# Features and keys by column, both ends reordered, and 64 spare transposes in the first tile, in a two-layer graph attention kernel

## The reference, cut to what matters

```python
def layer0(input, W, a, adj):
    h = input @ W
    e = leaky_relu((h @ a_src)[:, None] + (h @ a_dst)[None, :], 0.2)
    valid = (adj > 0) & (h.sum(axis=1) != 0)[None, :]
    att = softmax(where(valid, e, NEG), axis=1)
    L = valid.sum(axis=1)
    attention = where(att >= 1e-4, att, 0) * L[:, None]   # rows whose top is under 1e-4: 0
    return elu(h + attention @ h)

def layer1(qs, ks, adj):
    scores = leaky_relu(qs @ ks.T, 0.2)
    attn = softmax(where(adj > 0, scores, NEG_BIG), axis=1)
    return attn @ ks

x = layernorm(x + layer0(x, W, a, adj))
x = layernorm(x + layer1(x, ks, adj))
```

## Time and profile before

| | |
|---|---|
| median of 3 runs | 863.84 us (863.74 to 863.9) |
| the profiled execution, its time | 863.02 us |
| its span, first to last instruction | 861.2 us |
| TensorE busy, by matmuls | 825.6 us (96%) |
| VectorE busy | 787.5 us (91%) |
| ScalarE busy | 761.6 us (88%) |
| GpSimd busy | 223.2 us (26%) |

### The profile page before, as it was taken

One profiled execution on the slowest core, in us unless ns is written; L12 is line 12 of the kernel. 1 busy time (PEld: TensorE's weight loads), 2 busy tenths in 40 slices (PEclk: granted clock), 3 DMA queues, 4 the chain that ended last, 5 costly groups with the idle time before them and its releaser, 6 DMA issues.

```text
span 861.2 us, 17726 instructions
## 1 busy us (share of the span) xinstructions
PE 825.6 (96%) x7139; PEld 715.4 (83%) x7139; DVE 787.5 (91%) x1004; ACT 761.6 (88%) x731; POOL 223.2 (26%) x446
## 2 busy tenths in 40 slices
PE   6479999999999999999999999999999999999995
PEld 6368887888988888898888888988888898888885
DVE  3988999999999999999999999999999999999744
ACT  3978999999999999999999999999999999999653
POOL 2042133333222233321223233222233321222100
PEclk9699999999999999999999999999999999999998
DMA  9999866667787666678776666886766678620000
GB/s 213 235 130 171 149 97 122 129 132 138 152 153 107 126 125 131 133 148 153 132 115 122 130 131 139 154 152 103 127 127 128 136 149 154 101 41 22 5 1 10
DMA packets 39969, 106.07 MB, mean 123 GB/s; under 512 B 11088, under 2 KB 23504, under 8 KB 32208
## 3 DMA queue, kind: packets, MB, share of 16 engines
q0 software_dynamic: 20864, 66.06, 53.2%
q1 hardware_dynamic: 18592, 38.80, 12.7%
q10 hardware_dynamic: 432, 0.07, 0.0%
HBM read 138.48 MB, written 2.10 MB: 163 GB/s over the span
## 4 chain that ended last, share of the span: by engine, by line
PE 88%; DVE 5%; ACT 3%; issue 3%; DMA 1%; POOL 1%; ACTq 0%; POOLq 0%; DVEq 0%; SPq 0%
PE work L285 24%; PE sums L402 24%; PE sums L426 12%; PE sums L427 6%; PE work L373 6%; PE work L378 6%; PE work L374 6%; DVE att1T L816 1%; DVE att L805 1%; ACT att L587 1%; PE sums L432 1%; DMA a_sb<-a 1%; DMA mask_zero<-zero_cols 1%; PE work L310 1%; DVE att L766 1%
## 5 line engine op out<-in xcount | busy, mean ns | idle before, releaser
L285 PE MATMUL work<-ident,att 128*128 128x128 f32 x2072 | 258.4, 277 | 15.6 <-DVE att L917 11.9
L285 PEld LDWEIGHTS work<-ident,att 128*128 128x128 f32 x2072 | 236.3, 144 | 23.0 <-DVE att L917 12.1
L402 PE MATMUL sums<-h_all,att0T 128*128 128x128 f32 x2048 | 244.3, 275 | 0.0
L402 PEld LDWEIGHTS sums<-h_all,att0T 128*128 128x128 f32 x2048 | 236.2, 192 | 0.0
L426 PE MATMUL sums<-k_parts,att1T 128*128 128x257 f16 x1024 | 182.4, 274 | 1.2 <-DVE res L827 0.8
L427 PE MATMUL sums<-k_parts,att1T 128*128 128x129 f16 x1024 | 177.3, 218 | 0.0
L597 ACT ACTIVATE att1T<-work 128x1024 f16<-128x1024 f32 x128 | 130.9, 1027 | 36.3 <-PE work L285 36.3
L816 DVE SCALAR_TENSOR_TENSOR att1T<-work,att1T 128x1024 f16<-128x1024 f32 x128 | 152.4, 1211 | 5.1 <-ACT att1T L597 5.0
L805 DVE CUSTOM_DVE_ANT_0 att<-att,mask 128x2048 f32<-128x2048 f32 x64 | 146.4, 2290 | 2.4 <-ACT att L582 2.4
L766 DVE SCALAR_TENSOR_TENSOR att<-att,cut 128x2048 f32<-128x2048 f32 x62 | 145.4, 2349 | 0.0
L582 ACT ACTIVATE att<-work 128x1024 f32<-128x1024 f32 x128 | 127.4, 1026 | 19.4 <-PE work L378 19.4
(11 more groups left out here) (118 smaller groups left out, 653.2 us busy)
## 6 DMA issues: line engine op xcount, KB each, us to landing
mask<-adj POOLq DMA_DIRECT2D x31, 1024.0 KB, 8.6
mask_zero<-zero_cols SPq DMA_DIRECT2D x29, 1024.0 KB, 5.1
mask_zero<-adj POOLq DMA_DIRECT2D x29, 1024.0 KB, 11.6
att<-x SPq DMA_DIRECT2D x4, 512.0 KB, 6.7
k_parts<-ks POOLq DMA_DIRECT2D x2, 1024.0 KB, 18.0
x_sb<-x SPq DMA_DIRECT2D x32, 64.0 KB, 2.7
out<-x SPq DMA_DIRECT2D x32, 64.0 KB, 4.9
mask<-adj POOLq DMA_DIRECT2D x2, 512.0 KB, 6.7
```

Source lines behind the costliest of these rows:

```text
L285: mm = pe.transpose(place[:, b * P:(b + 1) * P], source(c * PER + b), ident[:, :])
L402: mm = pe.matmul(acc0, att0T[:, k * P:(k + 1) * P], h_all[:, k, :], start=(k == 0), stop=(k == BLOCKS - 1))
```

## The change

Six things are changed.

1. The host also passes `x` transposed (`xt`), the keys transposed (`kt`), the keys laid out as SBUF holds them (`ks_held`), and `a` as one row. `turn_x` and the copies `keep_x` are gone: SP loads `xT` at once. `turn_k`, `k_high_part`, `k_low_part` and SP's second load of the keys are gone: GpSimd loads `kt` with a cast (`kT_high`), VectorE negates it (`negate_kT`), and GpSimd adds `kt` in f32 to it (`kT_low`).
2. The three columns behind W come from one reduction and two multiply-reductions on VectorE, with `a` broadcast by DMA, in place of a transpose, a product and two copies.
3. The order ahead of the first tile and in the first slot is new on TensorE, ScalarE, VectorE and GpSimd. The third round of h goes from ScalarE to VectorE (`VECTOR_H` 3). GpSimd does `deviation0(0)` before `offset0(2)`, and issues the key's low half (`k_low`) before `add_adj(3)`.
4. TensorE transposes the identity 64 times into place 0 before `turn0(0, 0)`, once the last z has been copied.
5. The two early slots (tiles 1 and 2) are written out with another order on the three engines: ScalarE raises and bends tile 2 and 3 of layer 0 later, behind `raise1` and `copy1`.
6. The last two tiles have slots of their own. `sum1` of tile 30 stands behind all scores of tile 31 (half of it stood before them), and `sum1` of tiles 28 and 29 is spread otherwise. Tile 31 of layer 1 is masked and raised by quarters, and VectorE makes two of its four high halves (`BY_VECTOR`).

```diff
-        k_first = att1T[:, :].rearrange("p (b d) -> p b d", d=D)
-        x_all = att0[1][:, :].rearrange("p (b d) -> p b d", d=D)
         xT = att1
+        a_sb = att0[1][:, 0:2 * D]
...
-        FIRST = (("x", 0), ("x", 1), ("h", 0), ("x", 2), ("h", 1), ("x", 3), ("h", 2), ("z", 0), ("d", 0), ("h", 3),
-                 ("z", 1), ("d", 1), ("h", 4), ("z", 2), ("d", 2), ("h", 5), ("z", 3), ("d", 3))
-        FIRST_PLACES = SLOTS + 1
+        FIRST = (("h", 0, 0), ("h", 1, 1), ("h", 2, 2), ("z", 0, 3), ("d", 0, 0), ("z", 1, 2), ("h", 3, 1), ("d", 1, 3),
+                 ("h", 4, 0), ("h", 5, 1), ("z", 2, 2), ("d", 2, 3), ("z", 3, 0), ("d", 3, 1))
         H_PER = 6
-        VECTOR_H = 2
+        VECTOR_H = 3
         H_WIDE = D + 3
         H_FILLS = -(-BLOCKS // H_PER)
-        K_PLACE = (2, 0, 1, 2)
...
-            x_blocks = x.rearrange("(b p) d -> p b d", p=P)
             for c in range(CHUNKS):
-                part = slice(c * PER, (c + 1) * PER)
-                sp.dma_start(x_all[:, part, :], x_blocks[:, part, :]).then_inc(xall_in[c], 16)
-            sp.wait_ge(adj_in[1], 16)
-            sp.dma_start(k_first, ks.rearrange("(b p) d -> p b d", p=P)).then_inc(kall_in, 16)
+                sp.dma_start(xT[:, cols(c)], xt[:, cols(c)]).then_inc(xT_in[c], 16)
+            sp.wait_ge(first_adj_in[1], 16)
...
+                pe.wait_ge(w_in, 16)
+                pe.wait_ge(w_ready, 3)
+                pe.wait_ge(xT_in[c], 16)
...
-            pe.wait_ge(small_in, 48)
-            pe.transpose(wT_ps, w_sb[:, 0:D], ident[:, :]).then_inc(wT_made, 1)
-            first_fill(0)
-            pe.wait_ge(a_one_ready, 1)
-            pe.wait_ge(wT_ready, 1)
-            pe.matmul(v_ps, wT_sb[:, :], a_sb[:, :], start=True, stop=True).then_inc(v_made, 1)
-            for n in range(1, len(FIRST)):
+            for n in range(len(FIRST)):
...
-                    pe.wait_ge(kT_low, c + 2)
+                    pe.wait_ge(copied0, CHUNKS)
+                    pe.wait_ge(kT_high, 16)
+                    pe.wait_ge(kT_low, 16)
...
+            def turn_while_waiting():
+
+                wait_emptied("z", 3)
+                for b in range(64):
+                    pe.transpose(work[:, 0, (b % PER) * P:(b % PER + 1) * P], ident[:, :], ident[:, :])
+
             def first_slot():
-                for c in range(CHUNKS):
-                    turn0(0, c)
+                turn_while_waiting()
+                turn0(0, 0)
+                turn0(0, 1)
                 sum0(0, 0)
-                turn_k(0)
-                for c in range(1, CHUNKS):
-                    sum0(0, c)
-                for c in range(1, CHUNKS):
-                    turn_k(c)
+                turn0(0, 2)
+                turn0(0, 3)
+                sum0(0, 1)
+                sum0(0, 2)
+                sum0(0, 3)
                 turn_q(0)
-                for c in range(3):
-                    score(0, c)
+                score(0, 0)
+                score(0, 1)
+                score(0, 2)
...
+                t = TILES - 2
+                score(t - 1, 3)
+                for c in range(CHUNKS):
+                    turn0(t, c)
+                for c in range(3):
+                    sum0(t, c)
+                turn1(t - 1, 0, True)
+                sum0(t, 3)
+                sum1(t - 2, 2)
+                sum1(t - 2, 3)
+                for c in range(1, CHUNKS):
+                    turn1(t - 1, c, True)
+                turn_q(t)
+                sum1(t - 1, 0)
+                for c in range(CHUNKS):
+                    score(t, c)
+                t = TILES - 1
+                sum1(t - 2, 1)
+                turn0(t, 0)
+                sum1(t - 2, 2)
+                turn0(t, 1)
+                turn0(t, 2)
+                sum0(t, 0)
+                sum0(t, 1)
+                turn1(t - 1, 0, True)
+                turn0(t, 3)
+                sum0(t, 2)
+                sum0(t, 3)
+                sum1(t - 2, 3)
+                turn1(t - 1, 1, True)
+                turn1(t - 1, 2, True)
+                turn_q(t)
+                turn1(t - 1, 3, True)
+                for c in range(CHUNKS):
+                    score(t, c)
+                for c in range(CHUNKS):
+                    sum1(t - 1, c)
+                for c in range(CHUNKS):
+                    turn1(t, c, False)
+                for c in range(CHUNKS):
+                    sum1(t, c)
...
-            nc.scalar.dma_start(w_sb[:, 0:D], W).then_inc(small_in, 16)
-            for i in range(2):
-                nc.scalar.dma_start(a_sb[:, i:i + 1], a[i * D:(i + 1) * D, :]).then_inc(small_in, 16)
+            nc.scalar.dma_start(w_sb[:, 0:D], W).then_inc(w_in, 16)
+            nc.scalar.dma_start(a_sb, a.to_broadcast([P, 2 * D])).then_inc(a_in, 16)
...
-                keep_h(5)
+                for c in range(CHUNKS):
+                    copy0(0, c)
                 raise0(1, 0)
-                copy0(0, 0)
-                copy0(0, 1)
+                elu_exp(0)
                 raise0(1, 1)
-                copy0(0, 2)
-                k_high_part(0)
-                copy0(0, 3)
+                q_high_part(0)
                 bend0(2)
-                elu_exp(0)
-                k_high_part(1)
-                k_high_part(2)
-                q_high_part(0)
-                k_high_part(3)
+                for c in range(CHUNKS):
+                    bend1(0, c)
...
+                last_raise1(0)
+                last_raise1(1)
+                last_raise1(2)
+                copy1(t, 0)
+                copy1(t, 1)
+                last_raise1(3)
...
+            def last_mask1(k):
+                u = TILES - 1
+                dve.wait_ge(bent1, 4 * u + k + 1)
+                nc.vector.tensor_tensor_reduce(att1[:, quarter(k)], att1[:, quarter(k)], mask[u % MASKS][:, quarter(k)],
+                                               1.0, -3.0e38, ALU.add, ALU.max,
+                                               first_top[:, k:k + 1]).then_inc(masked1, 1)
+
...
+            def last_high1(c):
+                u = TILES - 1
+                dve.wait_ge(turned1, 4 * u + c + 1)
+                dve.wait_ge(summed1, 4 * (u - 1) + c + 1)
+                nc.vector.tensor_scalar(high1T[:, cols(c)], work[:, (2, 0, 1, 2)[c], :], LIFT, None,
+                                        ALU.mult).then_inc(last_copied1, 1)
...
+            dve.wait_ge(w_in, 16)
+            nc.vector.tensor_reduce(w_sb[:, D + 2:D + 3], w_sb[:, 0:D], AX.X, ALU.add).then_inc(w_ready, 1)
+            dve.wait_ge(a_in, 16)
+            for i in range(2):
+                nc.vector.tensor_tensor_reduce(x1[i][:, :], w_sb[:, 0:D], a_sb[:, i * D:(i + 1) * D], 1.0, 0.0,
+                                               ALU.mult, ALU.add, w_sb[:, D + i:D + i + 1]).then_inc(w_ready, 1)
...
+                zero_mask(1)
                 dve.wait_ge(first_topped, QUARTERS)
                 nc.vector.tensor_reduce(top0[0][:, :], first_top[:, :], AX.X, ALU.max).then_inc(masked0, 1)
                 first_offset0(0)
-                zero_mask(1)
                 mask0(1)
                 first_threshold0()
-                first_offset0(1)
-                for k in range(QUARTERS):
-                    first_cut(k)
+                negate_kT()
+                first_cut(0)
+                first_cut(1)
+                first_cut(2)
+                negate_k()
+                first_cut(3)
 
             def first_slot():
                 build_mask(2)
+                first_coefficient()
                 zero_mask(2)
+                first_offset0(1)
                 mask0(2)
-                first_coefficient()
-                k_low_part(0)
-                threshold0(1)
-                negate_k()
                 residual0(0)
                 elu(0)
-                k_low_part(1)
                 normalise0(0)
+                threshold0(1)
                 q_low_part(0)
-                k_low_part(2)
-                k_low_part(3)
                 cut(1, 0)
                 cut(1, 1)
...
+                last_mask1(0)
+                last_mask1(1)
+                last_mask1(2)
+                normalise1(t - 2)
+                last_mask1(3)
+                last_offset1()
+                finish1(t - 1)
+                for c in range(CHUNKS):
+                    if c in BY_VECTOR:
+                        last_high1(c)
+                    low_part1(t, c)
+                normalise1(t - 1)
+                finish1(t)
+                normalise1(t)
...
+            nc.gpsimd.dma_start(kT[:, 0, :], kt).then_inc(kT_high, 16)
             pool.wait_ge(k_one_ready, 1)
-            nc.gpsimd.dma_start(k_parts[:, :, D:2 * D], ks.rearrange("(b p) d -> p b d", p=P)).then_inc(k_high, 16)
+            nc.gpsimd.dma_start(k_parts[:, :, D:2 * D], ks).then_inc(k_high, 16)
             load_adj(2)
+            pool.wait_ge(kT_negated, 1)
```

(13 more changed lines are left out.)

## The result

The changed kernel takes 857.59 us (median of 4 runs, 856.89 to 858.25) against 863.79 us for the kernel before beside it (4 runs, 862.63 to 863.90): a ratio of 0.9931, with a 95% interval of 0.9914 to 0.9948, 6.2 us less. Beside later experiments it was 857.26 us, 0.9929 (0.9915 to 0.9943). The forecast was 856.7, range 852.0 to 860.6. The profiled execution took 856.99 us with a span of 855.2; the one before, 863.02 with 861.2.

| stretch | before | after | gained | forecast |
|---|---|---|---|---|
| start to tile 0's first score | 61.06 | 56.66 | 4.40 | 5.5 |
| to tile 3's first score | 76.14 | 75.11 | 1.03 | 1.2 |
| to tile 29's first score | 646.70 | 646.68 | 0 | 0 |
| to the last reciprocal | 71.56 | 70.94 | 0.62 | 0.5 |

What follows compares the result with a forecast made beforehand. TensorE was taken as busy from 150 to 750 us, with its waits at both ends. 863.02 less 5.5 (start), 1.2 (early slots) and 0.5 (end) gave 855.8; with the median 0.8 above, 856.7, range 852.0 to 860.6.

Steps and rivals of the forecast that it cites:

- The first product: Start: a's load lands at 5.5 us, so the first product of h starts at 6.4 instead of 11.24.
- First cut to `y`: Tile 0's start, all VectorE: 15.4 us instead of 16.0, `y` at 50.6, 0.6 us gained.
- `y` to x: Tile 0's start: 2.3 us of the former 5.84 go with `deviation0` in front, leaving 3.5.
- Spare transposes: Before tile 0's turns: 64 transposes worth nothing, `y` waits for VectorE; clock falls again, 2 us lost but hidden.
- Early slots: Tiles 1 and 2: three TensorE waits go, two of 0.4 us come, clock loss stays; net 1.2 us gained.
- Rival (5): `zero_mask(3)` waits for the third accumulation in one queue, landing at 83 against 2.3 us free: slower, 871.4; chance 0.06.
- the two signs of being wrong: Tile 0's start: TensorE being the last before `y`, or VectorE waiting for a DMA at `zero_mask(3)`.
- End: Tiles 30 and 31: exp wait and half clock go, but gaps before both `turn_q` and a late `turn1(31, 3)` leave 0.5 us.
- (1): Last tiles: the new gaps are filled and the end gives 4.9 us, not 0.5: 852.3; chance 0.20.
- (2): Before the first score: `kT_low` lands late, at 58, first score 2.4 us late: 859.1; chance 0.12.
- (3): Start: a's load comes behind x's, first product at 12.0, 5.6 later: 862.3, half of that likelier, 859.5; chance 0.11.
- (4): Early slots lose: TensorE waits 2 us in each of three slots: 863.4, no change; chance 0.06.

Runs made afterwards that it cites:

- The run with a ahead: Changed kernel with a's load issued first on SyncE's queue, ahead of the four loads of x, instead of second on ScalarE's: 856.43 us, ratio 0.9918.
- with `deviation0` behind: Changed kernel with GpSimd doing `offset0(2)` before `deviation0(0)` again: 857.01 us, ratio 0.9923.
- the refilled end: Changed kernel with `elu` before a low half in tile 30, last exp quarter before ScalarE's second copy, one high half back on ScalarE: 855.31 us, 0.99.
- the warm start: Changed kernel with 36 spare transposes put before the first product of h: 855.44 us, ratio 0.9907.
- with the keys late: Changed kernel with the keys negated behind `mask0(2)` and their low half issued after `add_adj(3)`, as in the kernel before: 858.12 us, 0.9927.

## Why the forecast held, step by step

**The first product: wrong.** Forecast 6.4, measured 8.43. The step that failed is a's landing, taken at 5.5 because its pieces had become fewer; it landed at 7.6, 6.5 us behind its issue beside the features, as late as the small loads before. The bound I had from that row, a first product at 8.0, was the better value. A load ahead of the features landed in 4.3 us. Of the 2.0 us only 0.9 reached the first cut, and that is partly luck: from the first product to the end of the last d it took 17.85 us and not 18.6, and from there to the cut 9.83 and not 10.2. The run with a ahead shows that little was lost by it: there tile 1's adjacency takes the place of a.

**The rounds of h**: forecast 6.55 us, measured 6.38, and 5.6 to 7.2 over the executions read. The last d ended at 26.28 instead of 25.0, the first cut came at 36.11 instead of 35.2: 1.67 us gained of 2.6.

**First cut to `y`**: forecast 15.4, measured 15.78. What it had not is that the issue on GpSimd stretches `build_mask(2)` by 0.76 (1.22 before, 1.98 now); the rest of the sum was 0.4 too long.

**`y` to x**: forecast 3.5, measured 3.16. The size was right, the reason wrong: I gave the gain to `deviation0` in front, and the moved issue alone has all of it (3.17 with `deviation0` behind). With `deviation0` in front and the issue late x came 4.43 us behind `y`. The two single edits and the kernel before told them apart.

**Spare transposes: right.** Forecast nothing, measured nothing in the span; the clock fell before tile 0's turns, as forecast. `y` waited for TensorE in no run. In the profiled execution it was near: the last sum ended at 51.20, `y` came at 51.89 behind `mask0(2)`, 0.7 us of room. The forecast had 2.8 before and 0.8 after the half clock, for which it took 2 us. With 112 spare transposes, at the full clock, the room was 2.9 us. The half clock cost 2.8 on the first turns and the first sum (3.67 and 3.19 us, 2.03 and 2.05 at the full clock), and 2.2 of it reached the last sum.

**Early slots**: forecast 1.2, measured 1.03. But the sum missed the load that now ends this stretch. Rival (5) named the mechanism, its place and its queue, gave 2.3 us of free room and a landing up to 83. Measured were a room of 1.3 us and a landing at 68.74, 1.25 late. So one of the two signs of being wrong that I had named came: VectorE waited for a DMA at `zero_mask(3)`. That the price is nothing is luck and not my sum, which had no landing of its own for the third load in a queue.

**`kT_low`**: landed 12.7 us behind its issue, no wait; the 11.6 of the earlier trace rows was the right neighbour.

**End**: forecast 0.5, measured 0.62, and 0.60 by the run that undoes it. TensorE's timeline has all three gaps that I had named, and the last is the late quarter of the exp, to the tenth as forecast:

```profile
801.28 0.33 PE L405 MATMUL sums<-ident,x 128*128 128x128 f32 x1 [0.66 <-DVE x L838]
...
826.36 0.33 PE L405 MATMUL sums<-ident,x 128*128 128x128 f32 x1 [0.84 <-DVE x L838]
...
842.61 1.09 PE L276 MATMUL work<-ident,att 128*128 128x128 f32 x8 [1.31 <-ACT att L585]
```

As idle time those before `turn_q` are 0.66 and 0.84, less than the 1.0 and 1.5 of the forecast, and all together are 3.0 with 0.18 before tile 31's first score. Idle time is not the whole loss, though. Read from the start of one group to the start of the next, and against the same groups elsewhere in the stretch (24 transposes 2.62 us, a tile's scores 5.17), 0.8 us are lost at the first, 1.6 around the second, 1.5 at the third, and the last sums take 0.3 longer than before. That is 4.2 of the 4.4 us forecast, and so the gain came out as it did for the reasons given.

**The rivals.** (1) fell: the end gave 0.6, not 4.9. (2) fell: `kT_low` was there in time. (3) came true by 2.0 of its 5.6 us at the first product, and 0.9 of that at the cut. (4) fell. (5) came true in its place and at no price.

The span came out 1.15 us longer than the sum has it: 1.1 too much forecast at the start, 0.9 of it by the first cut, 0.17 in the early slots, less 0.12 at the end. The median lies 0.6 above the profiled execution, where I had added 0.8.

## What to carry to other kernels

When two chains run side by side from the same event, as the sums and the third accumulation do from the first cut, compute both to their common end before pricing any speed-up of one; here a room of 1.3 us was all there was, and the 1.4 us gained by a faster clock were lost to it. A load's place in its queue is a price of its own: the same load landed at 54.6 and 58.1 us ahead of another, and at 68.7 behind it. Work added only to hold TensorE's clock paid here where the others wait for TensorE (2.2 us on the first products, 1.6 at the first cut), and in the two other places it didn't. And where a change moves an order and an issue together, undo each alone and both together: here the first two cost 0 and 1.3 us and both together, in the kernel before, 2.7, so the shares don't add up, and the total says nothing on which of them it was.

## What the runs showed of the hardware

The granted clock reads 1.00 from 7 to 14 us in all kernels read, while TensorE first does 6 to 7 instructions of 128 columns in one us there, and 11 or more later at the same reading. So at the start of an execution the record doesn't tell the clock; the count per us does. The us in which the count rises differs between executions (from 11 to 12 in the refilled end, from 13 to 14 in the changed kernel, from 14 to 15 with `deviation0` behind), and with it the three rounds of h, 5.6 to 7.2 us. In the warm start's run the spare transposes themselves run at 6 to 7 per us until 7 us, and at 11 from 8 us.

VectorE and GpSimd hold each other up. `build_mask(2)` takes 1.98 us beside the issue of the keys' low half, and 1.22 without; that issue takes 4.01 us there and 3.20 before. It is not so beside every issue: with the keys late, `build_mask(2)` took 1.22 us beside that of `add_adj(3)`. And GpSimd's `z_sum` and `rz` (0.29 and 0.57 us in the kernel before) take as long as VectorE's two cuts of 2.3 us beside them, in the changed kernel:

```profile
56.70 2.28 POOL L1216 TENSOR_SCALAR z_sum<-z 128x1 f32<-128x1 f32 x1
59.06 2.45 POOL L1219 TENSOR_TENSOR rz<-z_sum,minus_one 128x1 f32<-128x1 f32 x1
```

With `deviation0` behind, other two of GpSimd's scalars stand beside the cuts, `gate` and `coef`, and they are the long ones (2.46 and 2.22 us), while `z_sum` and `rz` take 0.29 and 0.57.

The Trainium skill, SBUF — State Buffer, section "Who interferes with whom", says that the two engines share one pair of ports, and that where both need it, whichever issues first has it for its whole instruction and the other is blocked. The second case agrees (2.28 against a cut of 2.3). In the first VectorE lost 0.76 us to an issue of 4 us, so it waited for a part of it only.

Three accumulations of 1 MB in one queue behind each other, issued within 7 us in the changed kernel, landed after 12.7, 20.1 and 25.7 us, while the loads of the same kind that stand alone take 11.8 in the median.
